# A decoder layer on one core: a denominator's products moved to GpSimd, and border steps reordered

## The chip, the cores and the metric

One Trainium2 chip, one of its cores. The time is that of the device for one execution of the program, in microseconds (us). TensorE (PE in the profile, with PEld its weight loads) does matrix products, VectorE (DVE), ScalarE (ACT) and GpSimd (POOL) work on rows, and SyncE (SP) issues most transfers. GpSimd and VectorE both work on operands in SBUF; TensorE writes PSUM banks ("bank").

## What is computed

The inputs are x and a context, both 16 x 64 x 512, float32. Three sublayers, each added to x:

```python
x = x + attn(layernorm(x))          # memory attention, no softmax
x = x + xattn(layernorm(x), ctx)    # 32 query heads, 4 key/value heads, keys from ctx and from the rows
x = x + ffn(layernorm(x))           # router over 64 experts, top 8, a bias per expert
...
sig_q = elu(q) + 1.0
q_sel = sig_q[:, :, ::G, :]         # every 4th head: 8 heads of 128
num = einsum('bshd,hde->bshe', q_sel, M)
den = einsum('bshd,hd->bsh', q_sel, z)[..., None] + EPS
output = repeat(num / den, G).reshape(b, s, H * D) @ Wo.T
```

The change concerns `den` (a sum over 128 features of sigma times z, for each row and head) and the order of work elsewhere.

## The kernel before

There are 1024 rows in 8 tiles of 128. Every float32 product is made of three matmuls of a high and a low part (`PARTS`); ScalarE rounds the high part (`high`, L1044) and VectorE subtracts it for the low part (`low`, L1364). Each engine has its own program text, in which the order of its work is written by hand, with semaphores between the engines; SyncE's transfers go in program order too, so a wait on SyncE holds up every later load.

The stages by the profile's time:

- to 67 us: transposes of the context and the weights, values, first keys.
- 67 to 178 us, **memory attention**. `memory_step(i)` goes through tile i // 2 and half i % 2 of the heads. TensorE makes the query Q(i) (L652), in the first steps also the folded product of M and `Wo` (`memory_weights`, L731, whose right side is `wofT`) and transposes (L714, L721), the output of step i - 4 (L798) and the transposes of the sigmas of step i - 2 (L765). VectorE adds the bias (qb, L1472), then makes for s = i - 1 four SCALAR_TENSOR_TENSOR with an accumulator (L1484: sig times z, summed into one of four columns of `rden`), adds epsilon (L1490), takes the reciprocal, and makes the next sigma from qb and ScalarE's exponential `qneg` (L1498). ScalarE scales the sigma by `rden`. GpSimd folds `Wo` over the four heads that share a memory head, with two adds for each of 8 memory heads (L565, L570), and takes the root of each layer norm (`root`, L554). After output tile t the row's layer norm makes `xn` and TensorE transposes it (`latent_transposes`, L643). The buffers `qneg`, `qb`, `kvout` serve before that as slots (`kv_slots`) of the 16 context keys on their way to memory: slot n % 3 for key n, and each user waits until the slot's last transfer is done.
- 178 to 222 us: latent values and keys from the new rows (L652, `save_latent_values`). The second set of their weights is cut into parts by `wkv_high(1)` and `wkv_low(1)`.
- 222 to 265 us: query pairs. A pair of heads is made with seven products of 2x2 block forms. The forms of the weights come from GpSimd's sums (`form_sums`, L581 to L589) of a loaded block `wq_raw`, ScalarE's and VectorE's parts (`direct_high/low` one part, `summed_high/low` three), counted by `form_hi` and `form_lo`, 4 per pair. The first `LEAD` + 1 pairs are made in a loop ahead of the attention steps, each later one within two steps. The block sums of the rows (`block_sum`, L1544) come first.
- 265 to 695 us: 32 attention steps (g, t), g a key/value head, t a tile: scores (L965), softmax (L1290, L1741, L1759), part of a query pair (L828) where there is one left, projection of the step before by `Wo` (`project`, L896, eight heads into bank 7), transposes of the probabilities (L991), the product with the values (PV, L1014). Per step VectorE makes the low parts of the transposed probabilities `pT` and of the outputs `oT`; at t = 0 of a new group also `wo_low` of eight heads. Steps from (2,7) have no pair left. In group 3 the router and the experts are added (router transposes L908).
- 695 us to the end: the last rows' router and experts.

In SyncE's text `load_pair(p)` waits until `form_lo` is 4 p, that is, until all low parts of pair p - 1 are made, since it overwrites `wq_raw`; in the first steps it stands ahead of the next step's key and query loads. In step (3,1) SyncE waits until `wo_lo` is 32 and then loads the router's weights and the expert biases over `wo_raw`:

```python
if t == 1:
    sp.wait_ge(wo_lo, KV * GH)
    sp.dma_start(rout_rows, router_w).then_inc(expert_loaded, 16)
```

## Time and profile before

| | |
|---|---|
| median of 3 runs | 720.72 us (719.7 to 722.87) |
| the profiled execution | 720.87 us, its span 719.1 us, mean granted clock 0.993 |
| TensorE busy | 692.9 us, 96% of the span |
| TensorE weight loads | 581.1 us, 81% |
| VectorE busy | 510.3 us, 71% |
| ScalarE busy | 349.5 us, 49% |
| GpSimd busy | 115.8 us, 16% |

The span is what the profiler saw of the one execution; what lies around it is 1.8 us. An engine counts as busy while one of its instructions runs; register, semaphore and DMA-issuing instructions do not count. In a row of the timeline, "[2.86 <-DVE wofT L1364]" says that the engine was idle for 2.86 us before this instruction and that VectorE's instruction on line 1364 ended the wait. The granted clock is TensorE's: 1.00 is 2.4 GHz, its lower level is 1.2 GHz.

### The profile page before, as it was taken

What the parts mean: (1) busy time and instruction counts of PE and PEld (TensorE: products, weight loads), DVE (VectorE), ACT (ScalarE), POOL (GpSimd) and SP (SyncE); (2) the same over time, 40 slices, a digit from 0 to 9 for tenths busy, and PEclk for the clock granted to TensorE, in tenths of its full rate; (3) what the DMA queues carried; (4) which work ended last, traced back from release to release, by engine and by line L of the source; (5) the groups of instructions that cost most, each with busy time, mean ns of one, the idle gap of its engine ahead of it and who ended that gap; (6) DMA issues with size and microseconds to landing.
All of it is one profiled execution on the core that took longest, in us unless ns stands there. A gap on an engine that the chain in (4) does not pass through costs nothing.

```text
span 719.1 us, 10998 instructions
## 1 busy us (share of the span) xinstructions
PE 692.9 (96%) x3562; PEld 581.1 (81%) x3562; DVE 510.3 (71%) x1078; ACT 349.5 (49%) x1042; POOL 115.8 (16%) x121
## 2 busy tenths in 40 slices
PE   8999699999999998999999999999999999899995
PEld 6888588887887787888888888888888888688874
DVE  2764877678725878677677876767977566778876
ACT  4454655456244446344445643554645336555541
POOL 0175400000101332020120220210202000022410
PEclk9999999999999999999999999999999999999998
DMA  9888510001234456543242833423542404221101
GB/s 329 296 288 286 205 59 1 1 0 59 88 118 143 135 170 206 189 147 100 77 126 80 263 102 102 146 87 110 194 146 78 146 31 154 75 82 59 59 16 58
DMA packets 69997, 90.14 MB, mean 125 GB/s; under 512 B 4224, under 2 KB 47232, under 8 KB 69952
## 3 DMA queue, kind: packets, MB, share of 16 engines
q1 hardware_dynamic: 64160, 80.13, 34.2%
q10 hardware_dynamic: 5792, 9.44, 3.7%
q8 instruction: 24, 0.39, 0.2%
q14 instruction: 21, 0.17, 0.1%
HBM read 62.29 MB, written 27.26 MB: 125 GB/s over the span
## 4 chain that ended last, share of the span: by engine, by line
PE 83%; DVE 8%; DMA 2%; issue 2%; ACT 2%; POOL 1%; SPq 0%; POOLq 0%; ACTq 0%; DVEq 0%
PE bank L896 23%; PE bank L828 19%; PE bank L652 14%; PE bank L965 7%; PE bank L1014 5%; PE bank L798 5%; PE bank L991 4%; PE bank L643 1%; DMA raw<-in_L_attn_Wo 1%; PE bank L765 1%; DVE regA L1364 1%; PE bank L687 1%; PE bank L731 1%; DVE forms L1364 1%; DMA raw<-in_ctx 1%
## 5 line engine op out<-in xcount | busy, mean ns | idle before, releaser
L896 PE MATMUL bank<-regA,oT 128*128 128x512 f32 x768 | 180.6, 391 | 3.1 <-DVE oT L1364 3.1
L896 PEld LDWEIGHTS bank<-regA,oT 128*128 128x128 f32 x768 | 143.4, 188 | 33.3 <-DVE oT L1364 3.9
L1290 ACT ACTIVATE probs<-bank,negmax 128x128 f32<-128x128 f32 x256 | 90.1, 378 | 46.0 <-DVE negmax L1741 46.0
L828 PE MATMUL bank<-xnT,forms 128*128 128x512 f32 x384 | 97.2, 397 | 0.2
L828 PEld LDWEIGHTS bank<-xnT,forms 128*128 128x128 f32 x384 | 70.1, 188 | 15.2 <-DVE qbuf L1571 1.7
L828 PE MATMUL bank<-regC,forms 128*128 128x512 f32 x288 | 75.8, 401 | 2.4 <-DVE qbuf L1571 2.4
L1044 ACT CAST oT<-bank 128x512 fp32r<-128x512 f32 x64 | 37.6, 588 | 79.3 <-PE bank L1014 76.5
L1044 ACT CAST pT<-bank 128x512 fp32r<-128x512 f32 x64 | 34.7, 592 | 69.5 <-PE bank L991 69.5
L652 PE MATMUL bank<-regC,xnT 128*128 128x512 f32 x256 | 67.8, 396 | 0.0
L965 PEld LDWEIGHTS bank<-k_ring,qbuf 128*128 128x128 f32 x512 | 62.0, 191 | 2.5
L828 PEld LDWEIGHTS bank<-regC,forms 128*128 128x128 f32 x288 | 52.8, 190 | 12.9 <-DVE qbuf L1571 2.4
L965 PE MATMUL bank<-k_ring,qbuf 128*128 128x128 f32 x512 | 62.2, 275 | 0.0
L581 POOL TENSOR_TENSOR diff<-wq_raw 128x256 f32<-128x256 f32 x16 | 11.8, 738 | 303.1 <-DVE forms L1364 303.1
L1364 DVE TENSOR_TENSOR pT<-bank,pT 128x512 fp32r<-128x512 f32 x64 | 41.4, 686 | 20.6 <-ACT pT L1044 20.5
L1290 ACT ACTIVATION_READ_ACCUMULATOR probs<-bank,negmax 128x1 f32 x256 | 55.3, 216 | 0.0
L652 PEld LDWEIGHTS bank<-regC,xnT 128*128 128x128 f32 x256 | 47.4, 188 | 9.4
L1759 DVE TENSOR_TENSOR probs<-probs,rrow 128x512 f32<-128x512 f32 x64 | 50.7, 792 | 2.2
L1364 DVE TENSOR_TENSOR oT<-bank,oT 128x512 fp32r<-128x512 f32 x64 | 43.5, 690 | 11.7 <-ACT oT L1044 11.5
L1014 PE MATMUL bank<-pT,v_ring 128*128 128x512 f32 x192 | 49.5, 392 | 2.3 <-issue 2.2
L798 PE MATMUL bank<-regB,regA 128*128 128x512 f32 x192 | 46.5, 392 | 0.0
L1014 PEld LDWEIGHTS bank<-pT,v_ring 128*128 128x128 f32 x192 | 35.6, 188 | 10.6 <-issue 2.7
L1735 DVE TENSOR_TENSOR resid<-resid,bank 128x512 f32<-128x512 f32 x31 | 21.2, 684 | 29.5 <-PE bank L896 29.5
(151 smaller groups left out, 1072.0 us busy)
## 6 DMA issues: line engine op xcount, KB each, us to landing
q_dram<-qbuf SPq DMA_DIRECT2D x32, 512.0 KB, 3.0
qbuf<-q_dram SPq DMA_DIRECT2D x31, 512.0 KB, 4.5
raw<-in_L_attn_Wo SPq DMA_DIRECT2D x8, 1024.0 KB, 7.6
raw<-in_L_xattn_Wo SPq DMA_DIRECT2D x4, 2048.0 KB, 9.9
wq_raw<-in_L_xattn_Wq SPq DMA_DIRECT2D x16, 512.0 KB, 4.1
k_ring<-keys_dram SPq DMA_DIRECT2D x32, 128.0 KB, 3.6
v_raw<-vals_dram SPq DMA_DIRECT2D x64, 64.0 KB, 3.5
rawk<-in_L_xattn_Wv SPq DMA_DIRECT2D x4, 512.0 KB, 4.0
```

The source lines that it names most:

```text
L652: last = nc.tensor.matmul(mm_bank(k)[:, :], left(a, c), right(b, c), start=i == 0, stop=i == len(terms) - 1)
L798: last = nc.tensor.matmul(y_bank(t)[:, :], sigT[:, a, m, (t % 4) * P:(t % 4 + 1) * P], memwo[:, b, m, :], start=m == 0 and i == 0, stop=m ...
L828: last = nc.tensor.matmul(k_bank[:, :], forms[:, p[1], a, i, c, :], right(b)[:, c, :], start=j == 0, stop=j == 5)
L896: last = nc.tensor.matmul(bank[7][:, :], oT[:, a, h, :], wo[:, b, h, :], start=h == 0 and i == 0, stop=h == GH - 1 and i == 2)
L965: last = nc.tensor.matmul(bank[bb][:, p * P:(p + 1) * P], q_ring[:, t % 2, p, bb, :, :].rearrange("p h s -> p (h s)"), k_ring[:, t % 4, :, ...
L991: last = nc.tensor.transpose(bank[bb][:, p * P:(p + 1) * P], probs[:, bb, p, :], ident[:, :])
L1014: last = nc.tensor.matmul(bank[4 + bb][:, :], v_ring[:, t % 2, bb, a, :], pT[:, bb, b, :], start=i == 0, stop=i == 2)
L1044: return nc.scalar.copy(dst, src)
L1290: last = nc.scalar.activation(probs[:, bb, p, :], bank[bb][:, p * P:(p + 1) * P], ACT.Exp, bias=negmax[:, bb, p:p + 1], accum_out=rowsum[: ...
L1364: return nc.vector.tensor_tensor(dst, src, high.bitcast(F), ALU.subtract)
L1735: nc.vector.tensor_tensor(rows, rows, bank[7][:, :], ALU.add).then_inc(proj_added, 1)
L1759: nc.vector.tensor_tensor(probs[:, bb, :, :], probs[:, bb, :, :], rrow[:, bb, :].unsqueeze(2).broadcast_to([P, 4, P]), ALU.mult).then_inc( ...
```

## The change

- The three slots of `kv_slots` are turned, so that ScalarE's first relu waits for key 14 and no more for key 15, and VectorE for the slot of `qb` alone; `kvout` is then written by GpSimd.
- `denominators(s)`: GpSimd multiplies sigma by z into `kvout`, 128x512, for each of 16 steps; VectorE's four instructions become one TENSOR_REDUCE. In VectorE's step the low part of the folded weights goes ahead of the reduction. Step 0's multiply stands between the folds of memory heads 6 and 7; roots are put between the later ones.
- The transposes (and their two parts) of latent tile 5 move from step 17 to step 18. The second weight set's high parts go behind value tile 2 (ScalarE), its low parts behind the last `x_low` (VectorE).
- The three summed forms of pair 5 move from the last turn of the lead loop into the first attention step, behind `v_high` and `v_low`.
- At t = 0 of groups 1 to 3 ScalarE makes `wo_high` 4 to 7 ahead of its oT casts. Where the step has no pair (group 3), VectorE makes `wo_low` 0, 1 ahead of its oT parts and 2, 3 behind them, and GpSimd makes 4 to 7, one after the other.
- In steps (2,7) and (3,1) TensorE projects heads 0 to 5 ahead of the transposes and heads 6 and 7 behind them.

SyncE's text is unchanged. The diff (a line of "..." where lines are left out):

```diff
@@ -191,7 +191,7 @@
-        kv_slots = (qneg[:, :], qb[:, :], kvout[:, :])
+        kv_slots = (kvout[:, :], qb[:, :], qneg[:, :])
@@ -251,6 +251,7 @@
         den_summed = sem("den_summed")
+        den_weighted = sem("den_weighted")
         rden_ready = sem("rden_ready")
@@ -559,7 +560,21 @@
+            def denominators(s):
+                pool.wait_ge(sig_ready, s + 1)
+                if s == 0:
+                    pool.wait_ge(rows_loaded, 32)
+                    pool.wait_ge(kv_written[0], kv_count(0, 16))
+                else:
+                    pool.wait_ge(den_summed, s)
+                nc.gpsimd.tensor_tensor(kvout[:, :].rearrange("p (m n) -> p m n", m=4),
+                                        sig[:, s % 3, :].rearrange("p (m n) -> p m n", m=4),
+                                        z_all[:, 4 * (s % 2):4 * (s % 2) + 4, :], ALU.mult).then_inc(den_weighted, 1)
             for m in range(MH):
+                if m == MH - 1:
+                    denominators(0)
                 pool.wait_ge(woa_loaded[m % 2], 16 * (m // 2 + 1))
@@ -569,7 +584,11 @@
                     .then_inc(fold_done, 1)
-            for k in range(2, 2 + NT):
+            for s in range(1, 2 * NT):
+                denominators(s)
+                if s >= 4 and s % 2 == 0 and s < 14:
+                    root(s // 2)
+            for k in range(7, 2 + NT):
                 root(k)
@@ -607,6 +626,11 @@
+            for h in range(4, GH):
+                pool.wait_ge(wo_hi, GH * (KV - 1) + h + 1)
+                pool.wait_ge(wo_lo, GH * (KV - 1) + h)
+                nc.gpsimd.tensor_tensor(wo[:, 1, h, :], wo_raw[:, h, :], wo[:, 0, h, :].bitcast(F), ALU.subtract)\
+                    .then_inc(wo_lo, 1)
             for t in range(1, NT):
@@ -782,8 +806,10 @@
                     wo_transposes(i + EARLY)
-                if output_in(i):
+                if output_in(i) and i != 2 * NT + 1:
                     latent_transposes(output_in(i) - 1)
+                if i == 2 * NT + 2:
+                    latent_transposes(output_in(i - 1) - 1)
@@ -884,12 +910,13 @@
-            def project(g, t, release):
+            def project(g, t, release, heads=range(GH)):
                 n = 8 * g + t
-                pe.wait_ge(oT_lo, 2 * n + 2)
-                pe.wait_ge(proj_added, n + 1)
-                for h in range(GH):
+                if heads[0] == 0:
+                    pe.wait_ge(oT_lo, 2 * n + 2)
+                    pe.wait_ge(proj_added, n + 1)
+                for h in heads:
                     if t == 0:
@@ -976,11 +1003,13 @@
                     product_4(pair)
+                divided = not pair and not (last_group and t >= 2) and t
+                front = range(GH - 2) if divided else range(GH)
                 if not first_step:
...
                     else:
-                        project(g, t - 1, False)
+                        project(g, t - 1, False, front)
                 if last_group and t >= 2:
@@ -1003,6 +1032,8 @@
                     product_3(pair)
+                elif divided:
+                    project(g, t - 1, False, range(GH - 2, GH))
                 pe.wait_ge(v_lo, n + 1)
@@ -1203,16 +1234,16 @@
-            act.wait_ge(kv_written[0], kv_count(0, 16))
+            act.wait_ge(kv_written[2], kv_count(2, 16))
             for i in range(2 * NT + 4):
...
                     wkv_high(0, wkv2, 2, 1, (2 * (i % 2), 2 * (i % 2) + 1))
+                if output_in(i) and i != 2 * NT + 1:
+                    latent_high(output_in(i) - 1)
                 if i == 2 * NT + 2:
-                    wkv_high(1, wkv2, 2, 0)
-                if output_in(i):
-                    latent_high(output_in(i) - 1)
+                    latent_high(output_in(i - 1) - 1)
@@ -1225,6 +1256,8 @@
                     latent_high(NT - 1)
+                if t == 2:
+                    wkv_high(1, wkv2, 2, 0)
                 if t == 4:
@@ -1240,7 +1273,8 @@
                 copy_1(p)
-                summed_high(p + 1, (p + 1) % 2)
+                if p < LEAD:
+                    summed_high(p + 1, (p + 1) % 2)
                 if p == 0:
@@ -1298,7 +1332,7 @@
                     v_high(g, t + 1)
-                if t % 2 and has_pair(g, t + 2):
+                if first_step or t % 2 and has_pair(g, t + 2):
                     summed_high(pair + 1, slot)
@@ -1314,15 +1348,15 @@
                     high(pT[:, bb, 0, :], bank[bb][:, :]).then_inc(pT_hi, 1)
-                for bb in range(2):
-                    act.wait_ge(pv_done, 2 * n + bb + 1)
-                    high(oT[:, 0, :, bb * S:(bb + 1) * S],
-                         bank[4 + bb][:, :].rearrange("p (h s) -> p h s", h=GH)).then_inc(oT_hi, 1)
                 if t == 0 and not first_step:
...
                         wo_high(g, h)
+                for bb in range(2):
+                    act.wait_ge(pv_done, 2 * n + bb + 1)
+                    high(oT[:, 0, :, bb * S:(bb + 1) * S],
+                         bank[4 + bb][:, :].rearrange("p (h s) -> p h s", h=GH)).then_inc(oT_hi, 1)
                 if t % 2 == 0 and has_pair(g, t + 3):
@@ -1472,25 +1506,19 @@
                                             bq_all[:, 4 * quad:4 * quad + 4, :], ALU.add).then_inc(mm_dve, 1)
+                if 1 <= i <= MH - EARLY:
+                    memory_weights(i + EARLY - 1)
                 if 1 <= i <= 2 * NT:
                     s = i - 1
-                    dve.wait_ge(sig_ready, s + 1)
                     r = rden[:, s % 2, :]
+                    dve.wait_ge(den_weighted, s + 1)
                     if s >= 2:
                         dve.wait_ge(sig_scaled, s - 1)
-                    for j in range(4):
-                        head = slice(j * P, (j + 1) * P)
-                        last = nc.vector.scalar_tensor_tensor(out=kvout[:, head], in0=sig[:, s % 3, head],
-                                                              scalar=1.0, in1=z_all[:, 4 * (s % 2) + j, :],
-                                                              op0=ALU.mult, op1=ALU.mult,
-                                                              accum_out=r[:, j:j + 1])
-                    last.then_inc(den_summed, 1)
+                    nc.vector.tensor_reduce(r, kvout[:, :].rearrange("p (m n) -> p m n", m=4),
+                                            axis=AX, op=ALU.add).then_inc(den_summed, 1)
                     dve.wait_ge(den_summed, s + 1)
...
                     nc.vector.reciprocal(r, r).then_inc(rden_ready, 1)
-                if 1 <= i <= MH - EARLY:
-                    memory_weights(i + EARLY - 1)
                 if i < 2 * NT:
@@ -1518,8 +1546,7 @@
             dve.wait_ge(rows_loaded, 32)
-            for r in (1, 2):
-                dve.wait_ge(kv_written[r], kv_count(r, 16))
+            dve.wait_ge(kv_written[1], kv_count(1, 16))
             for i in range(2 * NT + 4):
@@ -1527,13 +1554,14 @@
                     wkv_low(0, wkv2, 2 * KC, 1, (2 * (i % 2), 2 * (i % 2) + 1))
+                if output_in(i) and i != 2 * NT + 1:
+                    x_low(tr("latent", output_in(i) - 1), output_in(i) - 1)
                 if i == 2 * NT + 2:
-                    wkv_low(1, wkv2, 3 * KC, 0)
-                if output_in(i):
-                    x_low(tr("latent", output_in(i) - 1), output_in(i) - 1)
+                    x_low(tr("latent", output_in(i - 1) - 1), output_in(i - 1) - 1)
                 if output_in(i) is not None and i != 2 * NT - 1:
...
             x_low(tr("latent", NT - 1), NT - 1)
+            wkv_low(1, wkv2, 3 * KC, 0)
@@ -1646,8 +1674,8 @@
                     sum_11(p)
-                summed_low(p + 1, (p + 1) % 2)
                 if p < LEAD:
+                    summed_low(p + 1, (p + 1) % 2)
                     sum_u3(p)
@@ -1766,7 +1794,7 @@
                     v_low(g, t + 1)
-                if t % 2 and has_pair(g, t + 2):
+                if first_step or t % 2 and has_pair(g, t + 2):
                     summed_low(p + 1, slot)
@@ -1779,7 +1807,7 @@
                 if t == 0 and not first_step:
-                    for h in range(2 if p is not None else 0, 4):
+                    for h in range(2) if p is None else range(2, 4):
                         wo_low(g, h)
@@ -1801,7 +1829,7 @@
                 if t == 0 and not first_step:
-                    for h in range(4, GH):
+                    for h in range(2, 4) if p is None else range(4, GH):
                         wo_low(g, h)
...
```

VectorE's row of memory step 1 (the bias add into qb, the denominators, the folded weight's low part regB, the sigma, the parts of the transposed weights), before:

```order
L1472 TENSOR_TENSOR qb<-bank,rawk 128x512 [waits sig_ready,mm_done]
L1484 SCALAR_TENSOR_TENSOR kvout,rden<-sig,rawk 128x128 [waits sig_ready]
L1484 SCALAR_TENSOR_TENSOR kvout,rden<-sig,rawk 128x128 x3
L1490 TENSOR_SCALAR rden<-rden 128x4 [waits den_summed]
L1491 RECIPROCAL rden<-rden 128x4 [waits dve_step]
L1364 TENSOR_TENSOR regB<-bank,regB 128x512 [waits mm_act]
L1498 SCALAR_TENSOR_TENSOR sig<-qb,qneg 128x512 [waits qexp_ready]
L1364 TENSOR_TENSOR memT<-bank,memT 128x128 [waits tr_hi]
L1364 TENSOR_TENSOR wofT<-bank,wofT 128x512 [waits tr_hi]
```

and after the change:

```order
L1506 TENSOR_TENSOR qb<-bank,rawk 128x512 [waits sig_ready,mm_done]
L1398 TENSOR_TENSOR regB<-bank,regB 128x512 [waits mm_act]
L1517 TENSOR_REDUCE rden<-kvout 128x4 [waits den_weighted]
L1520 TENSOR_SCALAR rden<-rden 128x4 [waits den_summed]
L1521 RECIPROCAL rden<-rden 128x4 [waits dve_step]
L1526 SCALAR_TENSOR_TENSOR sig<-qb,qneg 128x512 [waits qexp_ready]
L1398 TENSOR_TENSOR memT<-bank,memT 128x128 [waits tr_hi]
L1398 TENSOR_TENSOR wofT<-bank,wofT 128x512 [waits tr_hi]
```

The four products are one reduction, which waits for GpSimd (`den_weighted`), and regB's low part has gone ahead of it.

VectorE's row at the end of the lead loop and the start of step (0,0) (forms are pair 5's low parts, the sum into qbuf is sum_11), before:

```order
L1364 TENSOR_TENSOR forms<-wq_raw,forms 128x512 [waits form_hi]
L1571 TENSOR_TENSOR u<-m,bank 128x512 [waits q_summed,q_copied,q_done]
L1364 TENSOR_TENSOR forms<-diff,forms 128x256 [waits form_hi]
L1364 TENSOR_TENSOR forms<-wq_raw,forms 128x512 [waits form_hi] x2
L1661 COPY stats<-meanvar 128x1
L1741 TENSOR_REDUCE negmax<-bank 128x4 [waits scores_done] x2
L1571 TENSOR_TENSOR qbuf<-m,bank 128x8x64 [waits q_kept,q_stored0,q_done]
```

and after the change, from the first maxima on:

```order
L1769 TENSOR_REDUCE negmax<-bank 128x4 [waits scores_done] x2
L1599 TENSOR_TENSOR qbuf<-m,bank 128x8x64 [waits q_kept,q_stored0,q_done]
L1599 TENSOR_TENSOR u<-u,bank 128x512 [waits q_summed,q_done]
L1785 RECIPROCAL rrow<-rowsum 128x4 [waits exp_done]
L1787 TENSOR_TENSOR probs<-probs,rrow 128x512 [waits rrow_ready]
L1785 RECIPROCAL rrow<-rowsum 128x4 [waits exp_done]
L1787 TENSOR_TENSOR probs<-probs,rrow 128x512 [waits rrow_ready]
L1599 TENSOR_TENSOR qbuf<-u,bank 128x8x64 [waits q_summed,q_done]
L1398 TENSOR_TENSOR v_ring<-v_raw,v_ring 128x2x128 [waits v_hi]
L1398 TENSOR_TENSOR forms<-diff,forms 128x256 [waits form_hi]
L1398 TENSOR_TENSOR forms<-wq_raw,forms 128x512 [waits form_hi] x2
```

The three low parts of pair 5 (one of diff, two of wq_raw) have left the place ahead of the first maxima and stand behind the probabilities and v_low (v_ring).

TensorE's row in step (3,1), from the last projected head ahead of the transposes to PV, before:

```order
L896 MATMUL bank<-regA,oT 128x512 [waits wo_lo]
L896 MATMUL bank<-regA,oT 128x512 x2
L991 MATMUL bank<-ident,probs 128x128 [waits probs_ready]
L991 MATMUL bank<-ident,probs 128x128 x3
L991 MATMUL bank<-ident,probs 128x128 [waits probs_ready]
L991 MATMUL bank<-ident,probs 128x128 x3
L908 MATMUL bank<-ident,raw 128x64 [waits q_summed,expert_loaded]
L908 MATMUL bank<-ident,raw 128x64 x3
L1014 MATMUL bank<-pT,v_ring 128x512 [waits oT_lo,pT_lo,v_lo]
```

and after the change:

```order
L1020 MATMUL bank<-ident,probs 128x128 [waits probs_ready]
L1020 MATMUL bank<-ident,probs 128x128 x3
L1020 MATMUL bank<-ident,probs 128x128 [waits probs_ready]
L1020 MATMUL bank<-ident,probs 128x128 x3
L935 MATMUL bank<-ident,raw 128x64 [waits q_summed,expert_loaded]
L935 MATMUL bank<-ident,raw 128x64 x3
L923 MATMUL bank<-regA,oT 128x512 [waits wo_lo]
L923 MATMUL bank<-regA,oT 128x512 x2
L923 MATMUL bank<-regA,oT 128x512 [waits wo_lo]
L923 MATMUL bank<-regA,oT 128x512 x2
L1045 MATMUL bank<-pT,v_ring 128x512 [waits oT_lo,pT_lo,v_lo]
```

Two heads of the projection (four rows of L923) now stand behind the router transposes (L935), ahead of PV (L1045).

## Rows read from the trace of the kernel before

**Rows 1.** Busy time by stretches: from:to, us, PE, PEld, DVE, ACT, POOL, clock, DMA, GB/s
```profile
67.00:92.00 25.00, 19.37 (x99) 15.60 (x97) 17.73 (x51) 13.51 (x32) 11.35 (x6) 1.00 0.65 225
92.00:160.00 68.00, 68.00 (x330) 56.48 (x329) 48.90 (x174) 34.25 (x81) 2.78 (x5) 1.00 0.02 6
...
272.00:276.00 4.00, 4.00 (x16) 3.36 (x16) 3.35 (x8) 2.56 (x12) 0.00 (x0) 0.57 0.87 305
```

**Rows 2.** Groups by line and form, GpSimd and VectorE: total, mean ns | idle before
```profile
L570 POOL TENSOR_TENSOR wofold<-raw 128x512 f32<-128x512 f32 x8 | 11.0, 1372 | 0.6
...
L597 POOL TENSOR_TENSOR v_ring<-v_raw,v_ring 128x256 fp32r<-128x256 f32 x6 | 6.8, 1138 | 85.2 <-ACT v_ring L1044 85.2
...
L605 POOL TENSOR_TENSOR raw<-raw,wq_raw 128x512 f32<-128x512 f32 x5 | 5.2, 1042 | 34.5 <-DVE wq_raw L1713 34.5
...
L1364 DVE TENSOR_TENSOR regA<-raw,regA 128x512 fp32r<-128x512 f32 x32 | 20.6, 685 | 0.0
...
L1484 DVE SCALAR_TENSOR_TENSOR kvout<-sig,rawk 128x128 f32<-128x128 f32 x64 | 17.0, 321 | 0.0
```

**Rows 3.** Timeline, 72 to 84 us: start, us, engine line op, [idle before <-releaser]
```profile
72.93 0.63 ACT L1186 ACTIVATE qneg<-qb 128x512 f32<-128x512 f32 x1 [4.90 <-DMA keys_dram<-qneg]
...
77.17 2.41 POOL L565 TENSOR_TENSOR raw<-raw 128x1024 f32<-128x1024 f32 x1 [0.79 <-DMA raw<-in_L_attn_Wo]
...
77.20 2.52 DVE L1484 SCALAR_TENSOR_TENSOR kvout<-sig,rawk 128x128 f32<-128x128 f32 x1
...
79.76 1.20 DVE L1490 TENSOR_SCALAR rden<-rden 128x4 f32<-128x4 f32 x1
...
83.29 0.47 PE L731 MATMUL bank<-wofT,memT 128*128 128x512 f32 x1 [2.86 <-DVE wofT L1364]
```

**Rows 4.** Timeline, end of the memory stage and the latent values
```profile
171.12 0.44 PE L643 MATMUL bank<-ident,xn 128*128 128x128 f32 x2 [1.13 <-DVE xn L1386]
...
186.19 1.23 DVE L1544 TENSOR_TENSOR qbuf<-xnT 128x1024 f32<-128x1024 f32 x1
...
195.65 0.68 DVE L1364 TENSOR_TENSOR forms<-wq_raw,forms 128x512 fp32r<-128x512 f32 x1
...
200.69 0.59 ACT L1114 COPY kvout<-bank 128x512 f32<-128x512 f32 x1 [0.27 <-PE bank L652]
```

**Rows 5.** Timeline of the first attention step, then a DMA issue with us to landing
```profile
269.88 0.38 SPq L444 DMA_DIRECT2D wq_raw<-in_L_xattn_Wq  x1
...
270.85 0.47 SPq L454 DMA_DIRECT2D qbuf<-q_dram  x1
...
271.71 2.27 PE L828 MATMUL bank<-regC,forms 128*128 128x512 f32 x6 [1.97 <-DVE qbuf L1571]
...
277.08 1.52 PE L828 MATMUL bank<-xnT,forms 128*128 128x512 f32 x6
...
279.81 0.27 PE L965 MATMUL bank<-k_ring,qbuf 128*128 128x128 f32 x1
...
qbuf<-q_dram SPq DMA_DIRECT2D x1, 512.0 KB, 5.7
```

**Rows 6.** ScalarE's oT group of the page, then the timeline of (2,7) to (3,1)
```profile
L1044 ACT CAST oT<-bank 128x512 fp32r<-128x512 f32 x64 | 37.6, 588 | 79.3 <-PE bank L1014 76.5
...
602.82 0.47 PE L1014 MATMUL bank<-pT,v_ring 128*128 128x512 f32 x1 [1.01 <-issue]
...
618.21 2.49 DVE L1364 TENSOR_TENSOR regA<-raw,regA 128x512 fp32r<-128x512 f32 x4
...
618.35 5.76 PE L896 MATMUL bank<-regA,oT 128*128 128x512 f32 x24 [1.34 <-DVE oT L1364]
...
620.73 0.50 SPq L532 DMA_DIRECT2D raw<-in_L_ffn_router_weight  x1
...
625.82 0.26 PEld L908 LDWEIGHTS bank<-ident,raw 64*128 64x128 f32 x3 [0.17 <-DMA raw<-in_L_ffn_expert_bias]
...
628.09 0.27 PE L965 MATMUL bank<-k_ring,qbuf 128*128 128x128 f32 x1
```

8 lines of the change are left out of this document (4 added, 4 removed).

## The prediction

> **What bounds the kernel now.** I read the page's busy shares first, which name TensorE (96%), then the busy time by stretches, then the idle gaps of TensorE in the timeline. From 92 to 160 us TensorE is busy 68.00 of 68.00 us at full clock while VectorE works 48.90 and GpSimd 2.78 [rows 1]: there a lighter VectorE buys nothing. What can move the end is the 26 us in which TensorE is not busy (719.1 - 692.9, the table above), most of it gaps at stage borders, and new gaps where the change delays somebody. So each edit is costed by what it does to the gap nearest to it.
>
> **GpSimd's price.** The multiply is 128x512 f32 with both inputs in SBUF; GpSimd's nearest row is the second fold add, 1.37 us; VectorE's subtraction of one `Wo` head, which GpSimd also gets, takes VectorE 0.685 us; its sums of products take 0.32 us per head, four per step [rows 2]. Second, the engines stop one another: the SCALAR_TENSOR_TENSOR that started at 77.20, just after GpSimd's 2.41 us fold at 77.17, took 2.52 us instead of 0.32, and a 128x4 TENSOR_SCALAR at 79.76 took 1.20 us, beside GpSimd's second fold add of the same block [rows 3]. I carry this as: a VectorE operation on SBUF alone waits out a GpSimd operation that began before it.
> The Trainium skill, "SBUF — State Buffer", section Who interferes with whom, calls this an exclusive lock that whoever starts first holds for its whole instruction, and says that tensor_reduce on this chip never contends. The first half agrees with the rows just named (2.52 and 1.20 us); no row shows a tensor_reduce from SBUF beside GpSimd. By the second half the sum itself is safe, but the TENSOR_SCALAR and the sigma behind it are not.
>
> **1. Entry of the memory stage (67 to 92 us).** Buffers turned: ScalarE's first relu waited 4.90 us until 72.93 for the last key store [rows 3]. The store it now waits for is one key earlier, so it can go some 2 us earlier: a gain of up to 2.2. But TensorE's gap there (2.86 us at 83.29, and one like it at 76.19) ends with VectorE's low part of wofT [rows 3]. VectorE's row ahead of it now holds: qb, the W low part (put ahead), the sum, which waits for GpSimd's multiply, epsilon, reciprocal, sigma, then wofT. The multiply of step 0 stands ahead of the last fold and behind m=6's two adds, ends near 77.8, and the last fold (2.41 + 1.28) then meets epsilon or sigma. I get 83.0 to 83.8 for that start against 83.29: **+0.2**, ends -2.2 and +1.0.
>
> **2. Steady memory steps.** Removed from VectorE: 4 x 0.321 = 1.3 us [rows 2]; added: one reduction of the same 512 columns, which I price as the subtraction of 512 columns, 0.685. GpSimd adds 16 x 1.37 = 22 us, in a stretch where it was busy 4%. In odd steps the multiply starts right behind the root of the layer norm and can hold up the TENSOR_SCALAR of xn by about 1.15 us; the chain has about that in hand. Cover: 68.00 of 68.00 busy TensorE [rows 1]. **0**; upper end 5 odd steps x 1.15 = +5.8 (rival 3), no gain possible.
>
> **3. End of the stage and latent values.** Transposes of latent tile 5 go one step later: the 1.13 us wait at 171.12 goes [rows 4], what is late next is tile 6, which keeps its date; net gain 0.7. But VectorE now does the second weight set's four low parts (4 x 0.685, behind ScalarE's four casts, which start only after value tile 2) right where it began its block sums at 186.19 [rows 4]. They begin at about 190.1: 3.9 later. Everything in line shifts by it: first forms' low part from 195.65 to 199.6, GpSimd's forms, ScalarE's casts, and the copy of value tile 7 that stood at 200.69 [rows 4] goes to 204.1. Its bank is wanted by the second latent key, which TensorE would reach at about 202.7: idle 2.05, less the 0.7: **+1.3**, ends -0.7 (all hidden) and +3.2 (3.9 less 0.7).
>
> **4. Pair 5's sums in the first step.** TensorE's 1.97 us gap at 271.71 is a wait for VectorE's sum_11, which stands behind three low parts of pair 5 [rows 5]. With these moved, sum_11 ends at about 269.0, and the six products behind it run at full clock: they took 2.27 us at half against 1.52 for six later. That would be -2.7. But the three low parts are also what SyncE's load of the next pair waits for (269.88), and the q load of the next step is queued behind it (270.85, landing 5.7 us later, at 276.6, ahead of its use at 279.81) [rows 5]. Pair 5's low parts now stand behind probs and v_low and end near 274.7; the pair's load goes at 274.75, q at 275.7, lands at **281.4**: the scores begin 1.65 later instead of 2.7 earlier. **+1.65**, ends -2.7 and +3.
> The Trainium skill, "DMA: Bandwidth & Descriptors", section Anatomy of one DMA, gives 2.0 us plus bytes over 436 GB/s, for this q load 3.2 us. The row has 5.7 (it shares the queues with the pair's load), and I go by the row. By the page q would land at 279, which is rival 2.
>
> **5. Step (2,7), projection divided.** Heads 6 and 7 fill the 1.01 us gap ahead of PV at 602.82 [rows 6]. The same heads cost the same. **-1.0**, ends -1.0 and 0.
>
> **6. Group 3's first steps.** VectorE did wo_low 4 to 7 in 2.49 us, ending 620.70, and SyncE issued the router's loads at 620.73, right behind; TensorE's router transposes waited 0.17 us for them at 625.82, 5.1 us later [rows 6]. So this chain is critical now already. In the new order VectorE's oT_low comes about 0.9 earlier (only two wo_low ahead of it; the gap of 1.34 before the projection shrinks by that), and its fourth low part is done at about 618.6. GpSimd then does four, each waiting for the one before. Its 256-column subtraction of this kind costs 1.14, its 512-column add 1.37 [rows 2]; with semaphores and probs beside it I take 1.7: done at 625.5. Lower end 4 x 1.04 (its fastest row of 512 columns [rows 2]), 622.9 with the waits; upper end 4 x 2.28 (twice the 256-column one), 627.8. Router transposes then at 625.5 + 5.1 = 630.6; behind them the divided step puts heads 6 and 7 (5.76 us for eight [rows 6], so 1.44) and PV; from the router transposes to the next scores it took 2.27 (625.82 to 628.09) [rows 6]. In groups 1 and 2 ScalarE's four `Wo` casts go ahead of its two oT casts as well; it idles 76.5 us in all before 64 of these, on TensorE's PV [rows 6], 2.4 per step, and the casts fill that: 0. Next scores 630.6 + 2.27 + 1.44 = 634.3 against 628.09: **+6.2**, ends +3.5 and +8.5.
>
> **7. Clock.** After the 1.97 us gap the granted clock fell to its lower level (0.57 mean from 272 to 276 [rows 1]), which costs 0.43 x 4.0 = 1.7. The 2.8 us gaps near 80 did not bring it down (1.00) [rows 1]. Two longer gaps are new (some 4.5 us ahead of 281.4, over 5 ahead of 630.6): I count one fall, **+1.7**, ends 0 and 3.4.
>
> Sum: 0.2 + 0 + 1.3 + 1.65 - 1.0 + 6.2 + 1.7 = +10.05. The profiled execution took 720.87 us, 0.15 over the median 720.72, so the forecast is **731**.
>
> **Rivals.** (1) The forecast, 727.5 to 735: chance 0.60. (2) **The first step keeps its gain**, q lands in time. For it: q's own bytes are few; against: its measured 5.7 us behind a pair's load. -2.7 for +1.65: 726.5. Chance 0.14. (3) **GpSimd becomes the bound of the memory stage**: multiply, root and xn block each other beyond TensorE's reserve, 5 x 1.15 = +5.8: about 736.5. For it: 2.52 for 0.32 us; against: GpSimd would be busy under half of the stage. Chance 0.12. (4) **Other side: the router load is not late.** The mechanism is the queue of SyncE behind GpSimd's four subtractions; faster than before only if they end by about 620.7, half a microsecond each (the nearest row has 1.14 for half the size), or if the load needs far less than 5.1 us. Then every gain stands: -2.2 - 0.7 - 2.7 - 1.0 - 0.9 = -7.5: 713.4. Chance 0.05. (5) **No change**: low price for GpSimd (+3.5) together with q in time: 0.2 + 1.3 - 2.7 - 1.0 + 3.5 = +1.3, 722.2. Chance 0.09. That the change does nothing at all is excluded by the moved instructions; that the multiply's move alone does nothing to the time is part of every case.
>
> **Numbers.** A measurement of this kernel tells 0.5% (3.6 us) from no change. Slower holds cases 1, 2, 3: 0.86. Same holds case 5: 0.09. Faster holds case 4: 0.05. The range runs from 723, which takes in case 2 and most of its spread, to 737, case 3.
>
> **What would show it.** Memory steps: TensorE still without gaps from 92 to 160. A DVE TENSOR_SCALAR of over 1 us beside GpSimd's multiplies. Block sums at about 190. SyncE's pair load at about 274.7 and a gap of 4 to 5 us of TensorE ahead of the scores at 281 (by absolute time 1 to 2 us later). No gap before PV in (2,7). GpSimd's four subtractions of 1.4 to 1.9 us, router loads issued near 625, a gap of over 5 us of TensorE released by these loads. Wrong it would be if those loads are issued before 622, or if the gap at the router transposes is under 2 us.

## The result, and the profile after

The changed kernel took 734.62 us (median of 4 runs, 733.64 to 735.28) against 720.34 for the kernel before on the same chip: 1.0184 times as long, 95% interval 1.0153 to 1.0216. It is slower, 14 us where 10 were forecast, inside the range. Run again beside the experiments below it took 733.80 us (6 runs) against 720.98: 1.0192 (1.0168 to 1.0216). The first profiled execution has a span of 733.5 us (before: 719.1); 2 us of this difference arise in the first 41 us, where the kernels are alike, and are absent from the second (span 731.1).

The busy time of the changed kernel by stretches (columns as in [rows 1]; stretches chosen around what was expected):

```profile
67.00:92.00 25.00, 21.78 (x101) 17.33 (x100) 16.24 (x26) 12.95 (x30) 15.09 (x9) 0.93 0.63 223
...
92.00:160.00 68.00, 67.85 (x327) 56.11 (x326) 51.20 (x98) 34.48 (x82) 16.84 (x16) 1.00 0.05 16
...
207.00:212.00 5.00, 4.73 (x14) 3.73 (x15) 0.46 (x1) 0.94 (x3) 0.00 (x0) 0.66 0.71 209
...
287.00:292.00 5.00, 4.76 (x23) 4.51 (x24) 1.90 (x4) 1.83 (x11) 0.00 (x0) 0.67 1.03 342
...
637.00:641.00 4.00, 3.94 (x12) 3.15 (x13) 0.36 (x1) 0.00 (x0) 0.00 (x0) 0.50 0.49 156
```

From 92 to 160 us TensorE is as full as before (67.85 of 68 against 68.00, [rows 1]) while GpSimd's work there rose from 2.78 to 16.84 us: the multiply's move neither helps nor hurts there. The last three stretches are at 0.66, 0.67 and 0.50 of full clock: the clock fell behind each of the three new gaps. It fell a fourth time at the entry (0.93 from 67 to 92 us, 0.59 from 78 to 82), behind a wait for wofT of 2.31 us. The kernel before has one fall in these parts of the program, at 272 us ([rows 1]), which is gone.

The groups of the moved and the held-up work, the last of them with its counterpart of the kernel before in the next fence:

```profile
L571 POOL TENSOR_TENSOR kvout<-sig,rawk 128x512 f32<-128x512 f32 x16 | 20.7, 1292 | 28.9 <-DVE sig L1526 28.9
...
L1526 DVE SCALAR_TENSOR_TENSOR sig<-qb,qneg 128x512 f32<-128x512 f32 x16 | 13.4, 840 | 5.3 <-ACT qneg L1219 5.0
...
L1517 DVE TENSOR_REDUCE rden<-kvout 128x4 f32<-128x512 f32 x16 | 10.8, 677 | 0.7 <-POOL kvout L571 0.6
...
L1420 DVE TENSOR_SCALAR xn<-resid,meanvar,rstd 128x512 f32<-128x512 f32 x8 | 9.2, 1146 | 5.3 <-POOL rstd L555 5.3
```

```profile
L1498 DVE SCALAR_TENSOR_TENSOR sig<-qb,qneg 128x512 f32<-128x512 f32 x16 | 11.4, 711 | 5.7 <-ACT qneg L1188 5.7
...
L1386 DVE TENSOR_SCALAR xn<-resid,meanvar,rstd 128x512 f32<-128x512 f32 x8 | 4.4, 547 | 5.3 <-POOL rstd L554 5.3
```

These means mix operations that met GpSimd with others that did not. Single rows of the changed kernel that met it:

```profile
79.16 2.39 POOL L580 TENSOR_TENSOR raw<-raw 128x1024 f32<-128x1024 f32 x1
...
79.98 0.68 DVE L1517 TENSOR_REDUCE rden<-kvout 128x4 f32<-128x512 f32 x1
...
107.79 1.29 POOL L571 TENSOR_TENSOR kvout<-sig,rawk 128x512 f32<-128x512 f32 x1
...
107.86 1.51 DVE L1420 TENSOR_SCALAR xn<-resid,meanvar,rstd 128x512 f32<-128x512 f32 x1 [0.67 <-POOL rstd L555]
```

Only one of the 16 reductions ran while GpSimd worked, the one at 79.98, wholly inside a fold, and it took its usual 0.68 us. Five of the eight layer norm operations (xn, input and output in SBUF) began 0.07 us behind a multiply and took 1.50 or 1.51 us, 0.96 more than the 0.55 us of the other three. Two of the 16 sigmas met a fold, at the entry (2.05 and 1.76 us); the others took 0.66 to 0.69. So blocking came where it was expected, and TensorE's reserve covered it in the steady steps.

The timeline of the changed kernel at its three new gaps:

```profile
190.02 2.50 DVE L1398 TENSOR_TENSOR tailC<-rawk,regC 128x512 fp32r<-128x512 f32 x4 [2.56 <-ACT regC L1075]
...
192.43 2.35 DVE L1572 TENSOR_TENSOR qbuf<-xnT 128x1024 f32<-128x1024 f32 x2
...
207.27 0.50 PE L676 MATMUL bank<-xnT,regC 128*128 128x512 f32 x1 [2.62 <-ACT qneg L1145]
...
280.77 0.38 SPq L445 DMA_DIRECT2D wq_raw<-in_L_xattn_Wq  x1
...
281.75 0.47 SPq L455 DMA_DIRECT2D qbuf<-q_dram  x1
...
287.24 0.58 PE L992 MATMUL bank<-k_ring,qbuf 128*128 128x128 f32 x1 [4.16 <-DMA qbuf<-q_dram]
...
626.23 6.09 POOL L632 TENSOR_TENSOR regA<-raw,regA 128x512 fp32r<-128x512 f32 x4 [73.21 <-DVE regA L1398]
...
629.88 1.32 DVE L1787 TENSOR_TENSOR probs<-probs,rrow 128x512 f32<-128x512 f32 x1
...
632.35 0.50 SPq L533 DMA_DIRECT2D raw<-in_L_ffn_router_weight  x1
...
637.06 0.36 PE L935 MATMUL bank<-ident,raw 64*128 64x64 f32 x1 [5.15 <-DMA raw<-in_L_ffn_expert_bias]
```

In order: VectorE's block sums begin at 192.43 (186.19 before, [rows 4]; 190.05 in the second trace, which lacks the late start), behind the four low parts of 190.02; the second latent key waits 2.62 us. SyncE issues the pair's load at 280.77 and the q load at 281.75 (269.88 and 270.85 before, [rows 5]); the scores of (0,1) wait 4.16 us for it. GpSimd's four subtractions take 6.09 us from 626.23, the router's loads are issued at 632.35, and the router transposes wait 5.15 us for them ([rows 6]: 620.73, and 0.17).

The way through the program can be read from the start of the scores of each attention step. The table gives it for the kernel before, and for the others how much later (+) or earlier they are than that, us, one trace each:

```text
step    before  change  again     e1     e2     e3     e4     e6     e7     e8     e9    e10    e11
(0,0)   265.07    6.12   3.24   2.99   2.86  -0.90   2.95  -0.31   2.51   4.86   2.09  -0.76   4.42
(0,1)   279.81    7.43   4.54   4.49  -0.15   0.92   4.27  -3.34  -0.52   6.28  -0.92  -3.77   5.53
(0,2)   294.75    9.02   6.28   7.39  -0.16   2.64   5.74  -3.35  -0.52   7.74  -0.93  -3.78   8.35
(2,7)   593.53    9.03   6.29   7.40  -0.15   2.65   5.74  -3.34  -0.52   7.75  -0.92  -3.77   8.36
(3,0)   604.28    7.77   5.03   6.14  -1.41   1.39   4.49  -4.60  -1.77   6.49  -2.18  -5.03   7.10
(3,1)   615.06    7.75   4.99   6.12  -1.42   1.35   4.45  -4.62  -1.81   6.47  -2.21  -5.05   7.06
(3,2)   628.09   14.39  11.89   8.63   6.16   8.42  11.15  -2.15  -0.81   9.96  -2.20  -5.04   8.21
(3,7)   686.32   14.40  11.96   8.64   6.19   8.45  11.14  -2.14  -0.82  11.17  -2.16  -5.08   8.27
```

From (0,2) to (2,7), 300 us, nothing changes to 0.02 us. The first line differs by up to 3.3 us between traces of the same code there (change, again, e1, e2, e8 and e11 are alike up to the first step), so differences between lines are read, not single figures. All of the loss lies in three places: up to (0,0), (0,0) to (0,2), and (3,1) to (3,2); (2,7) to (3,0) gains.

### The profile page after: what moved, and what is told of

Read it like the earlier page. It is cut to its first block, busy times and chain, and to the rows that moved or that the text cites. A ratio compares the mean times of both kernels' runs of the same rounds, so it can differ in the third digit from the quotient of the medians.

```text
span 733.5 us, 10921 instructions
## 1 busy us (share of the span) xinstructions
PE 700.4 (95%) x3562; PEld 586.7 (80%) x3562; DVE 512.7 (70%) x962; ACT 349.2 (48%) x1042; POOL 141.2 (19%) x141
## 4 chain that ended last, share of the span: by engine, by line
PE 79%; DVE 9%; DMA 4%; issue 3%; POOL 2%; ACT 2%; SPq 1%; ACTq 0%; POOLq 0%; DVEq 0%
PE bank L923 23%; PE bank L854 18%; PE bank L676 11%; PE bank L992 8%; PE bank L1045 5%; PE bank L824 5%; PE bank L1020 3%; PE bank L667 1%; DMA raw<-in_L_attn_Wo 1%; DMA keys_dram<-qneg 1%; PE bank L711 1%; PE bank L755 1%; PE bank L789 1%; POOL regA L632 1%; DMA qbuf<-q_dram 1%
## 5 line engine op out<-in xcount | busy, mean ns | idle before, releaser
L923 PE MATMUL bank<-regA,oT 128*128 128x512 f32 x768 | 182.6, 393 | 2.3 <-DVE oT L1398 1.9
L923 PEld LDWEIGHTS bank<-regA,oT 128*128 128x128 f32 x768 | 144.0, 189 | 33.0 <-DVE oT L1398 2.7
L992 PE MATMUL bank<-k_ring,qbuf 128*128 128x128 f32 x512 | 63.8, 279 | 4.2 <-DMA qbuf<-q_dram 4.2
L1045 PE MATMUL bank<-pT,v_ring 128*128 128x512 f32 x192 | 49.8, 395 | 1.2 <-issue 1.2
L1769 DVE TENSOR_REDUCE negmax<-bank 128x4 f32<-128x512 f32 x64 | 41.1, 682 | 5.4 <-PE bank L992 5.2
```

The source lines that it names most:

```text
L923: last = nc.tensor.matmul(bank[7][:, :], oT[:, a, h, :], wo[:, b, h, :], start=h == 0 and i == 0, stop=h == GH - 1 and i == 2)
L992: last = nc.tensor.matmul(bank[bb][:, p * P:(p + 1) * P], q_ring[:, t % 2, p, bb, :, :].rearrange("p h s -> p (h s)"), k_ring[:, t % 4, :, ...
L1045: last = nc.tensor.matmul(bank[4 + bb][:, :], v_ring[:, t % 2, bb, a, :], pT[:, bb, b, :], start=i == 0, stop=i == 2)
L1769: nc.vector.tensor_reduce(negmax[:, bb, :], bank[bb][:, :].rearrange("p (c n) -> p c n", c=4), axis=AX, op=ALU.max, negate=True).then_inc( ...
```

## The experiments

Ten kernels ran and the changed one again, with 4 to 12 timed runs each, in three groups (e1 to e4, e5 to e8, e9 to e11). The kernel before had medians of 721.04, 720.98 and 720.79 us in them, so medians of different groups are set side by side here. "Less than the changed kernel" is less than the 733.80 us of e5 ("again" in the table).

**e1: VectorE makes the low parts again** (behind oT_low all of 2 to 7).

```diff
-            for h in range(4, GH):
-                pool.wait_ge(wo_hi, GH * (KV - 1) + h + 1)
...
-                    for h in range(2, 4) if p is None else range(4, GH):
+                    for h in range(2 if p is None else 4, GH):
```

> The changed kernel with the last group's wo_low 4 to 7 back on VectorE (behind oT_low, after wo_low 2 and 3), everything else as changed, the divided projection too. Theory (GpSimd's four subtractions, 6.09 us for four in its trace, keep the router load back): the fourth is done about 3.6 us earlier, SyncE issues the router load about 3.6 us earlier, the gap of 5.15 us ahead of the router transposes shrinks to 0 to 1.5 us and the half-clock stretch behind it (637 to 641 us, about 2 us lost) goes: 6 to 7 us less than the changed kernel, 728 us. Rival (the divided projection itself costs, because heads 6 and 7 now stand behind the router load): under 3 us less, 732 or more.

Measured: 729.66 us, 4.1 us less than the changed kernel; (3,1) to (3,2) loses 2.5 us (6.12 to 8.63) instead of 6.6 to 6.9. So GpSimd's queue carried two thirds of the loss here, not all, and the 6 to 7 us expected did not come. VectorE and TensorE of this kernel:

```profile
623.18 3.69 DVE L1393 TENSOR_TENSOR regA<-raw,regA 128x512 fp32r<-128x512 f32 x6
...
626.78 1.28 DVE L1764 TENSOR_REDUCE negmax<-bank 128x4 f32<-128x512 f32 x2
...
630.00 0.66 PE L1015 MATMUL bank<-ident,probs 128*128 128x128 f32 x4 [2.33 <-DVE probs L1782]
```

The router's wait is gone, but the transposes now wait 2.33 us for the probabilities, since the maxima come behind six low parts, and the clock falls behind that gap as well. The order of the kernel before (four ahead of oT, four behind) hides the first four in the wait for oT.

**e2: the q load ahead of the pair's load.**

```diff
-            load_pair(LEAD + 2)
...
                     load_v(g + (t + 2) // 8, (t + 2) % 8)
+                if first_step:
+                    load_pair(LEAD + 2)
```

> The changed kernel with SyncE's load of the seventh pair moved behind the first step's key, query and value loads. Theory (the query load of step (0,1) waits in SyncE's queue for pair 5's low parts): the 4.16 us gap ahead of the scores of (0,1) goes, and the stretch at 0.67 granted clock behind it (about 1.6 us): 5.8 us less than the changed kernel, 728.8 us; the scores of (0,1) begin at about 283.1. Rival (the query load is late because its data is stored late, or it takes as long wherever it stands): the gap stays above 2 us and the time within 2 us of the changed kernel. Second rival: the pair's load, now later, makes the next forms late and a new gap comes in step (0,1) or (0,2): less than 3 us gained.

Measured: 727.13 us, 6.7 less than the changed kernel. (0,0) to (0,2) turns from +3.0 into -3.0 (2.86 to -0.16); the gap is gone and no other came. The queue on SyncE was the whole cause of this gap, and the moved sums are worth 3.0 us once it is out of the way. Ahead of the pair's load the q load took 4.1 us to landing.

**e3: the second weight set's parts back in step 18.**

```diff
                 if i == 2 * NT + 2:
+                    wkv_high(1, wkv2, 2, 0)
                     latent_high(output_in(i - 1) - 1)
...
-            wkv_low(1, wkv2, 3 * KC, 0)
```

> The changed kernel with the second weight set's high and low parts back in step 18, where they were before; latent tile 5's transposes stay moved. Theory (VectorE's block sums begin 3.9 us late because of the four low parts, and a chain of forms and copies ends in the second latent key): the 2.62 us gap at 207.3 goes and with it the stretch at 0.66 granted clock behind it (1.65 us): 4.3 us less, 730.3 us. Rival (the gap comes from latent tile 5's own move): unchanged within 1 us.

Measured: 731.81 us, 2.0 less by medians where 4.3 were expected (its 4 runs spread over 4.7 us, and the traced one is the fastest of them). The gap at the second latent key is gone, block sums begin at 185.83:

```profile
185.83 3.49 DVE L1571 TENSOR_TENSOR qbuf<-xnT 128x1024 f32<-128x1024 f32 x3
```

From the last latent transposes that follow a wait (177.67 in the kernel before) to the scores (0,0) it needs 88.07 us (87.73 to 88.64 in e6, e7, e9 and e10, which have this repair too), against 87.40 before and 92.22 and 91.70 in the changed kernel's two traces. But e1, e2, e4, e8 and e11 keep the late parts and the same gap of 2.61 or 2.62 us, and need only 90.09 to 90.57: TensorE's clock stayed full behind it there. In e4, where the gap ends at 206.16 (columns as in [rows 1]):

```profile
206.00:211.00 5.00, 4.84 (x21) 4.01 (x22) 0.35 (x1) 2.07 (x4) 0.00 (x0) 1.00 0.76 230
```

So, set against e3, the late parts cost 2.0 to 2.5 us in every trace, and the fall of the clock behind them another 1.1 to 2.1 us in two of seven traces only. The expectation had counted the fall as certain.

**e4: without GpSimd's multiplies.**

```diff
-                    nc.vector.tensor_reduce(r, kvout[:, :].rearrange("p (m n) -> p m n", m=4),
-                                            axis=AX, op=ALU.add).then_inc(den_summed, 1)
+                    for j in range(4):
+                        head = slice(j * P, (j + 1) * P)
+                        last = nc.vector.scalar_tensor_tensor(out=kvout[:, head], in0=sig[:, s % 3, head],
...
```

> The changed kernel without GpSimd's multiplies: VectorE makes its four products with accumulator per step again, the folded weight's low part stands behind them again, roots are where they were; buffers stay turned. Theory (the multiply's move is worth nothing in the steady steps, TensorE being busy 67.85 of 68 us there either way, and little at the entry): within 1.5 us of the changed kernel, 733 to 736 us. Rival A (GpSimd and VectorE block one another and this is part of the loss): 2 to 4 us less. Rival B (it did shorten the entry): 2 us or more above.

Measured: 732.15 us, 1.7 less than the changed kernel (1.5 were allowed for) and just below the 733 to 736 us expected; in the table it stands at 2.95 at (0,0), where kernels with the multiply and the same late parts have 2.86 to 6.12. Nothing is gained by the multiply's move. In the steady steps this is exact: from TensorE's start on wofT at 92.20 us in the kernel before to the latent transposes at 177.67, the twelve other traces take 84.86 to 84.92 us (85.47 before), with the multiplies or without.

**e5: the changed kernel again.**

> The changed kernel itself again, beside the others of this call, because the first 41 us of its first trace are 2 us longer than in the runs since then, in a stretch where the kernels do not differ. If that was chance: 732 to 733 us, spans by the table of score starts +12 to +13 behind the kernel before. If it belongs to the change: 734.5 again.

Measured: 733.80 us (6 runs, 732.89 to 737.71). The forecast of 732 to 733 us was missed by 0.8. The 2 us at the start of the first trace are absent from this one (and e11's trace has 3.1 us there), so they were chance; the medians of the two sets differ by 0.8 us.

**e6: the three repairs together** (e2, e3, and `wo_low` in its old order).

> The changed kernel with three edits put right: wo_low in its old order on VectorE (0 to 3 ahead of oT_low, 4 to 7 behind it), the seventh pair's load behind the first step's q load, the second weight set's parts back in step 18. Kept: turned buffers, GpSimd's multiplies, latent tile 5 later, pair 5's sums in the first step, divided projections. Theory (the loss is those three queues and the clock behind them; the rest is a gain): relative to the kernel before -0.3 at the entry, -2.9 in the first step, -1.25 at (2,7), 0 to -0.9 in (3,0) and (3,1): 5 us less than before, 716 us. The first try at wo_low (0, 1 ahead, 2 to 7 behind) left a gap of 2.33 us before the transposes of the probabilities, because VectorE's maxima stood behind six low parts; in the old order this gap should be 0.7. Rival (GpSimd's multiplies or the divided projection carry a loss of their own): 718.5 or more.

Measured: 718.75 us, 0.9968 of the kernel before (0.9949 to 0.9988). Under half of the expected gain of 5 us, and inside the rival's bound of 718.5 or more: the table holds -4.60 up to (3,0), as expected, but (3,1) to (3,2) gives 2.5 us back. TensorE there:

```profile
619.21 0.66 PE L1016 MATMUL bank<-ident,probs 128*128 128x128 f32 x4 [1.13 <-DVE probs L1782]
...
620.60 0.66 PE L1016 MATMUL bank<-ident,probs 128*128 128x128 f32 x4 [0.74 <-DVE probs L1782]
...
621.81 2.92 PE L919 MATMUL bank<-regA,oT 128*128 128x512 f32 x6
```

Dividing this projection opened a wait ahead of the transposes and put heads 6 and 7 (2.92 us for six matmuls) behind it at the lower clock; undivided, the eight heads cover the softmax. Not all of the 2.5 us is the divided projection's, see e7.

**e7: the repaired kernel without multiplies.**

> The repaired kernel without GpSimd's multiplies (VectorE's four products and the folded weight's low part as before). Theory (the multiply is worth nothing): within 1 us of the repaired kernel. Rival A (VectorE and GpSimd stop each other): 1.5 us or more less. Rival B (it shortens the entry, where the wait for wofT ends TensorE's gaps): 1 to 2.5 us more.

Measured: 717.73 us (9 runs), 1.0 less than e6; the runs of the two overlap (715.1 to 721.1, 716.4 to 721.5). Its trace has the same divided projection with the same gap, but at full clock:

```profile
622.03 0.66 PE L997 MATMUL bank<-ident,probs 128*128 128x128 f32 x4 [1.08 <-DVE probs L1770]
...
624.40 1.66 PE L900 MATMUL bank<-regA,oT 128*128 128x512 f32 x6
```

(3,1) to (3,2) gives back 1.0 us here (-1.81 to -0.81). So the divided projection itself costs 1.0 us, and the other 1.5 us in e6's trace are a fall of the clock behind a 1.13 us gap that does not come every time.

**e8: the changed kernel, (3,1) undivided.**

```diff
-                divided = not pair and not (last_group and t >= 2) and t
+                divided = not pair and not last_group and t
```

> The changed kernel with the projection of step (3,1) undivided again (all eight heads ahead of the transposes), that of (2,7) still divided. Theory (heads 6 and 7 now stand behind the router load, in the open, 1.44 us at full and about 1.9 us at the granted clock of 0.5 there; undivided they fit into the 5 us gap, their low parts being done at the time at which the load is issued): 1.5 to 2 us less than the changed kernel. Rival (the transposes of the probabilities then wait for heads 6 and 7 and push PV out by the same): no difference.

Measured: 732.34 us, 1.5 less, as expected. Its gap at the router transposes is 2.83 us instead of 5.32 ("again"): the two heads went into it. (3,1) to the last steps costs 4.7 us instead of 7.0, part of it behind the scores of (3,2), which still ran at the lower clock.

**e9 and e10: repaired and undivided, with and without multiplies.**

> The repaired kernel with the projection of step (3,1) undivided again, that of (2,7) still divided. Theory: with the low parts on VectorE the router load is in time, the eight heads cover the time until the first probabilities, and dividing only opens a gap of 1.13 us ahead of the transposes and puts heads 6 and 7 (2.92 us there, at the lower clock) behind them. The way from the scores of (3,1) to those of (3,2) falls from 15.50 us to the 13.0 of the kernel before: 2.5 us less than the repaired kernel, 716.3 us. Rival: the gaps are of the chain of the softmax and stay; under 1 us less.

> The same without GpSimd's multiplies. Theory (the multiply is worth nothing): within 1 us of the kernel beside it, and if anything less, 716 us. Rival (the multiply shortens the entry): 1.5 us more.

Measured: e9 718.20 us, 0.9950 (0.9925 to 0.9974) of the kernel before; e10 716.06 us, 0.9943 (0.9915 to 0.9971). The step (3,1) to (3,2) is back at the old length (-2.21 to -2.20, -5.05 to -5.04), so the gaps were not the softmax's own, as the rival had it. But e9 is only 0.6 us under e6 by the medians, where 2.5 were expected: 1.5 of these were e6's fall of the clock, and in the traced execution the entry of e9 is worse. TensorE, VectorE and GpSimd of e9 there:

```profile
77.44 1.29 POOL L572 TENSOR_TENSOR kvout<-sig,rawk 128x512 f32<-128x512 f32 x1
...
78.69 2.34 POOL L581 TENSOR_TENSOR raw<-raw 128x1024 f32<-128x1024 f32 x1
...
78.77 0.69 DVE L1512 TENSOR_REDUCE rden<-kvout 128x4 f32<-128x512 f32 x1 [1.68 <-POOL kvout L572]
...
79.49 1.57 DVE L1515 TENSOR_SCALAR rden<-rden 128x4 f32<-128x4 f32 x1
...
81.19 1.74 DVE L1521 SCALAR_TENSOR_TENSOR sig<-qb,qneg 128x512 f32<-128x512 f32 x1
...
83.87 0.76 PE L751 MATMUL bank<-wofT,memT 128*128 128x512 f32 x1 [4.83 <-DVE wofT L1393]
```

Here GpSimd waited 2.3 us for the data of a fold ahead of these, step 0's multiply followed at 77.44, the reduction waited 1.68 us for it, and epsilon (1.57 us) and sigma (1.74) were blocked by the last fold: 4.83 us of gap. e8 has the same (GpSimd waits 2.06 us, the gap is 5.06). From the start behind TensorE's first wait for wofT to the start behind its second (76.19 and 83.29 us before, so 7.10), the other seven traces with the multiply need 6.62 to 6.64 us, those without 6.98 to 7.14, e8 and e9 9.30 and 9.06. The two traces of the changed kernel have a second wait of only 0.78 us where the other five have 2.40, but not because less was waited for: the clock had just fallen, TensorE's work between took longer, and the 6.62 us are the same. From the second wait to 92.20 it turns around: 9.64 or 9.65 us with the multiply at full clock (change, again, e2, e3, e11), 8.97 without it (e10; 8.91 before). So at full clock the multiply and the order that came with it gain 0.4 us and lose 0.7 at the entry, and in two of nine traces, where a fold's data came late, they lose 2 more. Over the pairs (changed and e4, e6 and e7, e9 and e10) the kernels without multiplies are 1.7, 1.0 and 2.1 us shorter by medians; the runs overlap in all three pairs (in the first by 0.02 us), and the falls of the clock differ too. That the move costs a little is therefore likely, not proven.

**e11: GpSimd's subtractions freed.**

```diff
-                pool.wait_ge(wo_lo, GH * (KV - 1) + h)
-                    .then_inc(wo_lo, 1)
+                    .then_inc(wo_lo_pool, 1)
```

> The changed kernel with GpSimd's four subtractions of the last group freed from their wait for VectorE's low parts (a semaphore of their own; each begins when ScalarE's high part is there). Theory: GpSimd could start about 4.5 us earlier, at the first high part instead of behind VectorE's fourth low part; four at 1.5 us end 3.5 to 4.3 us earlier, the router load with them, the gap of 5.3 us falls to 1 to 2 and the lower clock behind it goes: 5 to 6 us less than the changed kernel, 728 us. Rival (blocking): VectorE's two low parts there (both inputs in SBUF) and GpSimd's subtractions stop one another, oT_low comes 1.5 to 3 us later and opens a gap ahead of the projection: 2 to 3 us less only.

Measured: 727.93 us, 5.9 less than the changed kernel; (3,1) to (3,2) costs 1.15 us instead of 6.9. Both theories are in the rows:

```profile
620.93 5.91 POOL L633 TENSOR_TENSOR regA<-raw,regA 128x512 fp32r<-128x512 f32 x4 [68.58 <-ACT regA L1079]
...
621.68 2.77 DVE L1402 TENSOR_TENSOR regA<-raw,regA 128x512 fp32r<-128x512 f32 x2
...
625.71 4.79 PE L927 MATMUL bank<-regA,oT 128*128 128x512 f32 x18 [1.64 <-DVE oT L1402]
...
628.01 0.50 SPq L535 DMA_DIRECT2D raw<-in_L_ffn_router_weight  x1
```

GpSimd starts at 620.93 and the loads go at 628.01, 4.3 us earlier than at 632.35 (3.6 us, counted from the scores of (3,1) in each trace), and the router's gap is gone. And it blocks: VectorE's first two low parts take 2.77 us instead of 1.28, oT comes later and the projection waits 1.64 us. VectorE's other two, behind oT, take 2.40 us and end at 627.97, after GpSimd's last (626.84), so it is they that now release the loads. The chain's wait for VectorE, with the fall of the clock behind the gap, cost 5.7 us of the 6.9; what is left, 1.15 us, is nearly all the divided projection, which costs 1.0 in e7.

## Why the prediction was right, and where its sum was off

The forecast was 10.05 us over the kernel before; the second trace of the changed kernel has 12.0 (731.1 against 719.1). The steps are read from the column "again" and five more marks: TensorE's matmuls that begin at 41.39, 92.20, 177.67 and 203.21 us in the kernel before come 0.27, 0.50 and 1.06 us earlier and 1.68 later, and the router transposes 8.67 later (634.49 against 625.82):

```text
step of the prediction                      forecast   measured
start (same code)                               0        -0.3
1 entry, to 92 us                             +0.2       -0.2
3 latent tile 5 later, to 178 us              -0.7       -0.6
3 gap at the second latent key                +2.0       +2.7
4 first step, to the scores of (0,1)          +1.65      +1.3
5 (2,7)                                       -1.0       -1.3
6 up to the router transposes                 +4.8       +3.7
6 heads 6, 7 behind them                      +1.44      +1.0
7 lower clock, behind the three gaps          +1.7       +5.5 (1.6, 1.7, 2.2)
```

The way from the router transposes to the scores of (3,2) is 5.49 us in this trace and 2.27 before. It is 3.27 and 3.21 in e7 and e11, which have heads 6 and 7 there at full clock, so 1.0 of the 3.2 us is the heads' and 2.2 the clock's.

**Step 7** is the term that was mis-sized: one fall was counted, and three that cost time came. Each new gap (2.62, 4.16, 5.15 us) was followed by some 4 to 5 us at 0.50 to 0.67. The gap of step 3 was left out of this count, and of the two longer ones only one was taken, for which no reason is given beyond the pair of 2.8 us gaps near 80 us that did not bring the clock down. The runs show that such a gap decides nothing either way: in the changed kernel a wait of 2.31 us there did bring it down (at no cost, since it only shortened the next wait, see e9), and behind the 2.62 us gap it fell in two traces of seven. The two longer gaps, of 3.96 to 5.62 us in all traces, were followed by a fall every time: these two should have been counted in full, and the third as a chance.

The total came out near for a mixed reason: the clock was 3.8 us short, and step 6 was 1.5 us too high. Of the clock's 5.5 us, 1.6 are a fall that does not come in every execution.

**Step 6**: right in its chain, somewhat high in its price: 1.52 us from one subtraction to the next, not 1.7, of which GpSimd works 1.41, and VectorE's probabilities (1.32 us instead of 0.69 for one) were held up as GpSimd's neighbours. e1 and e11 show that it is the start behind VectorE's fourth low part, and not GpSimd's pace alone, that made the load late. What the prediction had not seen is that the divided projection of (3,1) is a loss even with the load in time (1.0 us in that step at full clock, e7 against e10; 2.5 with a fall, e6 against e9).

**Step 4**: right to 0.35 us, and the reason is proven by e2. The q load took 5.2 us from its issue at 281.75 (5.7 in [rows 5]); by the Trainium skill's sum for one DMA ("DMA: Bandwidth & Descriptors", Anatomy of one DMA), an estimate of 3.2 us, TensorE would have waited 2 us less. That section gives its sum for transfers that GpSimd issues, and this one is SyncE's, behind two others, so the prediction was right to go by the row; ahead of the pair's load it took 4.1 us (e2).

**Step 3**: the mechanism is proven by e3, the gap was 2.62 instead of 2.05; the block sums began at 190.05 in the second trace, where 190.1 was forecast.

**Steps 1 and 2**: the sum was near nothing both ways, as forecast. The xn operation was held up by 0.96 us in five steps, where 1.15 was the bound, and the reserve held. The Trainium skill's rule ("SBUF — State Buffer", Who interferes with whom) agrees with these traces in both halves: operations with two SBUF inputs and TENSOR_SCALAR wait until GpSimd's instruction ends, and the reductions that met a fold did not wait (0.68 us in the changed kernel, 0.69 at 78.77 in e9).

Rival 2 (the first step keeps its gain) fell, and e2 shows its size: 6.0 us between the two cases, 4.35 as forecast plus one fall of the clock. Rival 3 fell with the full stretch from 92 to 160 us. Rival 4's 713.4 us counted 2.2 us at the entry that no trace shows over its whole length (the most is 1.2, in e11, up to 92.20); with the router load in time the best kernel has 716.06 (e10).

## What to carry to other kernels

When work goes to a slower engine, follow what waits for its last result: here the loads in SyncE's queue behind `wo_lo` and `form_lo` cost more than all computing that was moved. Price a new gap of TensorE together with the stretch at the lower clock behind it, as certain where gaps of that length always had one, and as a chance where they had it in some traces. One trace is then not enough to price an edit: two of the savings first read here (e3, e9) held a fall of the clock that the edit had not caused. Where the engine relieved was not the bound (VectorE at 49 of 68 us), relieving it earns nothing, and the blocking of two engines on SBUF can make the rest depend on when transfers land (e8, e9).
